# A mixture-of-experts kernel: first-choice results go through a buffer in the order of the second choices, and the output is written once

## What is computed

```python
# gnn: x + gnn(layernorm(x), adj), 128 graphs of 64 nodes, D = 128, H = 512
x = x + _L0_gnn_ref(_layernorm(x), adj, ...)
# ffn on the 8192 tokens: 8 experts, two of them per token
gate_logits = xf @ Wg + bg
top_w, top_i = jax.lax.top_k(gate_logits, 2)
top_w = jax.nn.softmax(top_w, axis=-1)
w_dense = jnp.sum(jax.nn.one_hot(top_i, E) * top_w[..., None], axis=1)
out = jnp.zeros_like(xf)
for e in range(E):
    h = jax.nn.gelu(xf @ W1[e] + b1[e], approximate=False)
    out = out + w_dense[:, e:e + 1] * (h @ W2[e] + b2[e])
```

## Time and profile before

| | us |
|---|---|
| median of 3 runs | 489.01 (488.24 to 489.42) |
| the profiled execution | 488.13 |
| its span in the trace | 486.2 |
| busy PE, PEld | 465.9 (96%), 422.8 (87%) |
| busy DVE, ACT, POOL | 354.1 (73%), 264.2 (54%), 353.4 (73%) |
| chain that ended last | PE 67%, POOL 15%, issue 14% |
| mean granted TensorE clock | 0.987 of full |

### The profile page before, as it was taken

The page is one execution under the profiler, slowest core; times in us unless marked ns, Lnnn a source line. Parts: engine busy times, 40 slices in busy tenths (PEclk is TensorE's granted clock), DMA queues, the critical chain, the costliest instruction groups (busy, mean ns, idle before and its releaser), DMA issues.

```text
span 486.2 us, 14184 instructions
## 1 busy us (share of the span) xinstructions
PE 465.9 (96%) x3715; PEld 422.8 (87%) x3715; DVE 354.1 (73%) x1484; ACT 264.2 (54%) x830; POOL 353.4 (73%) x310
## 2 busy tenths in 40 slices
PE   8999999999999999999999999999999999999960
PEld 6788888778888777899999999999999999999950
DVE  6798888888887675888867777777667676776730
ACT  2333333333333324677777777777777777777730
POOL 3232587877778777777777777777588888888884
PEclk9999999999999999999999999999999999999995
DMA  6995122222222212323334333333254555555430
GB/s 188 361 320 168 56 79 73 79 77 64 68 64 68 78 40 74 86 70 90 96 91 108 100 104 98 93 85 99 47 68 68 72 72 76 70 69 73 56 33 5
DMA packets 54436, 44.78 MB, mean 92 GB/s; under 512 B 9506, under 2 KB 46024, under 8 KB 54360
## 3 DMA queue, kind: packets, MB, share of 16 engines
q1 hardware_dynamic: 36480, 26.11, 20.0%
q0 software_dynamic: 16592, 17.13, 17.5%
q10 hardware_dynamic: 1288, 0.62, 0.4%
HBM read 25.49 MB, written 19.25 MB: 92 GB/s over the span
## 4 chain that ended last, share of the span: by engine, by line
PE 67%; POOL 15%; issue 14%; DVE 1%; ACT 1%; POOLq 1%
PE ps L683 14%; PE ps L668 14%; POOL out_y L440 14%; PE ps L589 11%; PE ps L575 10%; PE ps L541 3%; PE ps L549 3%; PE ps L582 3%; PE ps L557 2%; PE ps L661 2%; PE ps L567 1%; POOL dispatched_rows L425 1%; PE ps L500 1%; POOLq L71 1%; PE ps L612 0%
## 5 line engine op out<-in xcount | busy, mean ns | idle before, releaser
L775 ACT ACTIVATE gelu_t<-ps,block_w 128x128 f32<-128x128 f32 x568 | 162.5, 369 | 35.1 <-PE ps L668 34.7
L425 POOL DMA_INDIRECT dispatched_rows<-payload,row_idx x128 | 126.0, 985 | 37.3 <-issue 36.7
L668 PE MATMUL ps<-slot_t,block_w 128*128 128x128 f32 x1136 | 150.1, 275 | 0.6 <-ACT slot_t L769 0.6
L683 PE MATMUL ps<-experts,gelu_t 128*128 x1136 | 150.3, 275 | 0.4 <-ACT gelu_t L775 0.3
L683 PEld LDWEIGHTS ps<-experts,gelu_t 128*128 128x128 f32 x1136 | 138.2, 192 | 0.8 <-issue 0.8
L668 PEld LDWEIGHTS ps<-slot_t,block_w 128*128 128x128 f32 x1136 | 138.0, 192 | 0.9 <-ACT slot_t L769 0.9
L440 POOL DMA_INDIRECT out_y<-y_out,slot_rows x71 | 112.6, 1586 | 23.3 <-issue 23.3
L437 POOL DMA_INDIRECT out_y<-y_out,slot_rows x71 | 72.2, 1017 | 24.1 <-issue 19.0
L1115 DVE TENSOR_TENSOR y_bias<-ps,block_w 128x128 f32<-128x128 f32 x142 | 41.3, 291 | 52.8 <-PE ps L683 48.1
L1029 DVE COPY block_w<-experts 128x644 f32 x142 | 73.6, 519 | 2.0 <-issue 2.0
L1035 DVE TENSOR_SCALAR slot_n<-slot_rows 128x128 f32<-128x128 f32 x142 | 58.5, 413 | 15.5 <-DMA slot_rows<-dispatched_rows 15.1
(11 more groups left out here) (146 smaller groups left out, 413.3 us busy)
## 6 DMA issues: line engine op xcount, KB each, us to landing
slot_rows<-dispatched_rows SPq DMA_DIRECT2D x142, 66.5 KB
xs<-in_x SPq DMA_DIRECT2D x16, 256.0 KB, 6.5
xs_t<-in_x_t SPq DMA_DIRECT2D x16, 256.0 KB, 3.1
experts<-in_f_w SPq DMA_DIRECT2D x16, 256.0 KB, 5.3
out_y<-y_out,slot_rows POOLq DMA_INDIRECT x142, 3.2
adj_in<-in_adj_t SPq DMA_DIRECT2D x16, 128.0 KB, 4.3
dispatched_rows<-payload,row_idx POOLq DMA_INDIRECT x128, 2.4
dispatched_rows<-pad_rows SPq DMA_DIRECT2D x18, 66.5 KB
```

Source lines behind the costliest of these rows:

```text
L425: pool.indirect_dma_start(rows[k], bass.IndirectOffsetOnAxis(row_idx[:, g, j * TOP_K + k:j * TOP_K + k + 1], 0), payload[:, g * JT + j, 0: ...
L668: mm = pe.matmul(bank((2 * i + c // 2) % FH_BANKS, c % 2 * SLOTS, SLOTS), block_w[:, i % BLOCKS, c * P:(c + 1) * P], slot_t[:, i % 2, :], ...
L683: mm = pe.matmul(bank(Y_BANK + i % 2, 0, P), gelu_t[:, i % 2, c, :], experts[:, bass.ds(at + (OW2 + c * P), P)], start=(c == 0), stop=(c = ...
L775: act.activation(gelu_t[:, i % 2, c, :], ps[:, (2 * i + c // 2) % FH_BANKS, c % 2 * SLOTS:(c % 2 + 1) * SLOTS], ACT.Gelu, bias=block_w[:, ...
```

## The change

The payload gets one more number: PLACE, the row of the token's second choice. VectorE copies it from row_f in place_rows. A new DRAM tensor, first_results, has the rows of the second choices' regions, 128 numbers each. A first-choice tile's result (x2 included) is scattered by POOL to the rows PLACE of first_results and no longer to out. A second-choice tile loads from first_results the same 128 rows as from dispatched_rows 1, so that each row meets the earlier result of its token (SyncE, load_prior, into prior, a ring of 16 in the memory of xs, which is free by then). VectorE adds it: take_second brings the result with its bias from PSUM to y_out, and close_second multiplies by the weight and adds the prior rows. POOL then scatters to out with a plain write; every row of out is written once. wait_written is gone; in its place SyncE issues load_prior of tile 71 only behind the slots of tile 86, which wait for the write of tile 70. So that VectorE need not stand at once, the closings of tiles 71 to 77 are put off: tile 71 is closed behind the taking of tile 74, then two at a time, and from tile 78 on each tile behind its own taking.

```diff
-TOKEN, WEIGHT, MEAN, RSTD, X2 = 0, 1, 3, 4, 5
+TOKEN, PLACE, WEIGHT, MEAN, RSTD, X2 = 0, 1, 2, 4, 5, 6
...
+        first_results = nc.dram_tensor("first_results", (DUMMY + SLOTS, P), F32).ap()
...
+        prior = xs[:, 0:RING, :]
...
                 sp.dma_start(rows[g // E][bass.ds(end, SLOTS), :], pad_rows[:]).then_inc(padded, 16)
+                if g >= E:
+                    sp.dma_start(first_results[bass.ds(end, SLOTS), :], pad_rows[:, X2:WID]).then_inc(padded, 16)
...
+            def load_prior(i, first):
+                q = (i - TILES) % RING
+                sp.dma_start(prior[:, q, :], first_results[bass.ds(first, SLOTS), :]).then_inc(prior_loaded[q], 16)
...
-            for i in range(TILES, NT):
-                load_slots(i)
+            firsts = [load_slots(i) for i in range(TILES, TILES + RING)]
+            for i in range(TILES, TILES + RING):
+                load_prior(i, firsts[i - TILES])
+            for i in range(TILES + RING, NT):
+                load_prior(i, load_slots(i))
...
                 if i < TILES:
+                    place = bass.IndirectOffsetOnAxis(slot_rows[:, r, PLACE:PLACE + 1].bitcast(I32), 0)
+                    pool.indirect_dma_start(first_results, place, y_out[:, r, :], None, bounds_check=DUMMY - 1,
+                                            oob_is_err=False).then_inc(added[r], 16)
+                else:
+                    token = bass.IndirectOffsetOnAxis(slot_rows[:, r, TOKEN:TOKEN + 1].bitcast(I32), 0)
                     pool.indirect_dma_start(out, token, y_out[:, r, :], None, bounds_check=T - 1,
                                             oob_is_err=False).then_inc(added[r], 16)
-                else:
-                    pool.indirect_dma_start(out, token, y_out[:, r, :], None, bounds_check=T - 1,
-                                            oob_is_err=False, compute_op=ALU.add).then_inc(added[r], 16)
...
-                if TILES - 8 <= i < TILES - 1:
-                    wait_written(2 * i - TILES)
-                    wait_written(2 * i - TILES + 1)
-                if i == TILES:
-                    wait_written(TILES - 2)
-                    wait_written(TILES - 1)
...
+                dve.tensor_copy(payload[:, cols(g), PLACE].bitcast(I32),
+                                row_f[:].rearrange("p (j k) -> p j k", k=TOP_K)[:, :, 1])
...
+            def take_second(i):
+                r = i % RING
+                dve.wait_ge(y_done, i + 1)
+                after(dve, added[r], 16 * (i // RING))
+                dve.tensor_tensor(y_out[:, r, :], ps[:, Y_BANK + i % 2, 0:P],
+                                  block_w[:, i % BLOCKS, OB2:OB2 + P], ALU.add).then_inc(y_chain, 1)
+            def close_second(i):
+                r, q = i % RING, (i - TILES) % RING
+                dve.wait_ge(y_chain, i + 1)
+                dve.wait_ge(prior_loaded[q], 16 * ((i - TILES) // RING + 1))
+                dve.scalar_tensor_tensor(y_out[:, r, :], y_out[:, r, :],
+                                         slot_rows[:, r, WEIGHT + 1:WEIGHT + 2], prior[:, q, :],
+                                         ALU.mult, ALU.add).then_inc(y_ready, 1)
...
+                if i < TILES:
+                    finish(i)
+                else:
+                    take_second(i)
+                if i == TILES + 3:
+                    close_second(TILES)
+                if TILES + 4 <= i < TILES + 7:
+                    close_second(2 * i - TILES - 7)
+                    close_second(2 * i - TILES - 6)
+                if i >= TILES + 7:
+                    close_second(i)
```

More of the change, by code:

```diff
@@ L252, in moe_gnn @@
         added = [sem(f"added{r}") for r in range(RING)]
+        prior_loaded = [sem(f"prior_loaded{r}") for r in range(RING)]
         def q_bank(g):
@@ L331, in _ @@
                 sp.dma_start(rows[k][DUMMY:DUMMY + SLOTS, :], pad_rows[:]).then_inc(padded, 16)
+            sp.dma_start(first_results[DUMMY:DUMMY + SLOTS, :], pad_rows[:, X2:WID]).then_inc(padded, 16)
             def pad(g):
@@ L342, in load_slots @@
                              rows[i // TILES][bass.ds(first, SLOTS), :]).then_inc(slots_loaded[r], 16)
+                return first
+            def load_prior(i, first):
+                q = (i - TILES) % RING
+                sp.dma_start(prior[:, q, :], first_results[bass.ds(first, SLOTS), :]).then_inc(prior_loaded[q], 16)
             sp.wait_ge(early_table_ready, 1)
@@ L362, in _ @@
             sp.wait_ge(tables_ready, 1)
[L363 removed]
+            sp.wait_ge(padded, 16 * (E + TOP_K + 1))
             sp.wait_ge(late_dispatched, 16 * JT * (G - EARLY_GROUPS))
@@ L1119, in finish @@
                 row = slot_rows[:, r, :]
-                weight = row[:, WEIGHT + k:WEIGHT + k + 1]
-                if k == 0:
-                    m = dve.scalar_tensor_tensor(y_out[:, r, :], y_bias[:, i % 2, :], weight, row[:, X2:WID],
-                                                 ALU.mult, ALU.add)
-                else:
-                    m = dve.tensor_scalar(y_out[:, r, :], y_bias[:, i % 2, :], weight, None, ALU.mult)
-                m.then_inc(y_ready, 1)
+                dve.scalar_tensor_tensor(y_out[:, r, :], y_bias[:, i % 2, :], row[:, WEIGHT:WEIGHT + 1],
+                                         row[:, X2:WID], ALU.mult, ALU.add).then_inc(y_ready, 1)
+            def take_second(i):
+                r = i % RING
+                dve.wait_ge(y_done, i + 1)
[9 more added lines that the diff above has]
+                                         ALU.mult, ALU.add).then_inc(y_ready, 1)
             take_x2(G - 1)
@@ L1132, in _ @@
                     norm_slots(i + AHEAD)
+                if TILES < i < TILES + 8:
+                    dve.wait_ge(y_chain, i)
                 if i + 3 < NT:
```

10 lines of the change are left out of this document (2 added, 8 removed).

## The result

| | before | changed | forecast |
|---|---|---|---|
| median, us | 489.12 (16 runs, 487.3 to 492.1) | 486.87 (16 runs, 483.2 to 487.87) | 481.3 (478.8 to 485.5) |
| ratio | | 0.9937, 95% from 0.9916 to 0.9958 | 0.984 |
| profiled execution, span | 488.13, 486.2 | 486.89, 485.0 | 480.4, 478.5 |
| busy PE, DVE, POOL, us | 465.9, 354.1, 353.4 | 469.1, 353.0, 311.7 | POOL 40 less |
| mean granted clock | 0.987 | 0.989 | |

The change makes the kernel faster, by 0.6% and not by 1.6%; the time lies above the range.

A forecast was written before the change was run, and what follows sets the result against it. TensorE's matmuls set the floor, with POOL's delayed scatters behind the last one; -8.8 - 0.4 + 1.1 + 0.2 + 0.2 = -7.7 us against the 489.01 median gave 481.3, range 478.8 to 485.5.

The forecast's parts named there:

- terms a and b: Before the second choices: VectorE's copy of the place, +0.2 (0 to 0.2); eight more pad loads on SyncE, +0.2 (0 to 1).
- the new wait at the switch: VectorE waits 3.3 us for tile 71's prior rows, making TensorE about 1.0 late: +1.1 us (0 to 3.2).
- The accumulate goes, and POOL's waits with it: 71 POOL scatters each 0.57 us shorter; POOL catches up, last scatter starts at 470.45 in place of 479.28: -8.8 us.
- The rival of the clock: At the switch, TensorE still for 4.4 us drops to 1.2 GHz; ten slow tiles give about 504 us, slower; chance 0.03.
- The 4.2 us between the last landing and the end I leave as they are: End of the span: the 4.2 us after the last scatter's landing was assumed unchanged.
- The -0.4: Last scatter, issue to landing: plain write 2.4 us in the median, accumulate 2.7; -0.4 us (between -0.3 and -0.6).
- Rival 5: VectorE's closings and POOL's scatters lock each other, each waiting up to 0.98 us; about 507 us; chance 0.02.
- Rival 4: Second-choice scatters on POOL: plain costs as much as accumulating, nothing is caught up; 487 to 489 us; chance 0.03.
- term c: 71 prior-row loads on SyncE, 1.6 us a tile against 1.895, twelve tiles ahead of need: 0, covered by slack.

The follow-up runs named there:

- experiments 1 to 5: Six variants of the changed kernel: closings put off (one or four tiles more), pad loads moved, both edits, dummy matmuls, another SyncE load order; 482.51 to 489.03 us.
- before_plain: Kernel before with plain scatters for all second choices, waits kept, the addition of the two results left out; 482.84 us, ratio 0.9861.
- prior_early: Changed kernel with SyncE loading slots 71 to 80, waiting for the last six first-choice writes, then loading priors 71 to 80, then pairs from 81; 485.86 us.
- late_pads: Changed kernel with the eight pad loads of first_results moved behind the slot loads of tiles 71 to 78; 489.03 us, ratio 0.9991.
- defer7: Changed kernel with closings put off four more tiles: tile 71 closed behind the taking of tile 78; 482.51 us, ratio 0.9855.

## Why the forecast missed

The forecast span was 478.5, the changed kernel's is 485.0. The 6.5 us between, by the steps of the prediction:

| step | forecast | measured | of the 6.5 |
|---|---|---|---|
| first part, with terms a and b | +0.4 | +1.28 (taking of tile 71 at 338.86 for 337.58) | 0.9 |
| the new wait at the switch | +1.1 | +4.16 | 3.1 |
| last result to last scatter | 0.98 after the last taking | 1.56 | 0.6 |
| last scatter's start to the end | 6.9 - 0.4 = 6.5 | 8.5 | 2.0 |

1. **The accumulate goes, and POOL's waits with it** held: POOL 41.7 us less busy, last scatter nearly behind the last result. One term was too small: I took 0.30 from the last result to the last scatter, which is the step between two scatters in a backlog. POOL starts 0.79 after a result that it waits for, and here the scatter of tile 140, which runs until 476.17, makes it 0.88.
2. **The new wait at the switch** is the step that failed. The place was right, and VectorE's wait for the load is what stops TensorE; the size was a quarter of what was measured. Of the 3.1 us between, about 1.0 is the longer stop of TensorE (1.96 for 1.0), 1.7 is the clock, which I had left out of this term (see 3), and 0.4 is the rest, the wait for the weight copy above all. Two terms under the stop were wrong. I let SyncE be idle at tile 86's place in the ring, so that the landing of tile 70's write set the time (slots of 86 at 344.6); it came to them with six slot loads behind one another and issued them at 346.29, about 0.9 of the 1.7 by this backlog, 0.8 because the write itself started later (342.25 for 341.44). And I took 1.87 from issue to use where 2.8 was needed, inside my bounds (3.87); in the other profiles in which VectorE waited for this load it took 1.94 to 2.98. In the changed kernel the issuing instruction alone took 1.25, where that of the first prior load took 0.33 in all six kernels of experiments 1 to 5; nothing shows why. Together the load was usable 2.7 later than forecast; 1.2 of it is hidden, as VectorE too came later.
3. **The rival of the clock** was put in the wrong place. I wanted a gap of 4.4 us, from the one fall that the trace showed, and priced it at ten tiles of half speed. The runs show a fall behind a gap of 1.96 and one behind 3.46, each over after 3.4 us, at 1.7 us. A rival that costs 1.7 and is seen behind a stop of 2 belonged inside the main case, whose own gap was 1. The page "TensorE: Matmul & The Clock Gate" of the Trainium skill, section "Part 1: The HAM clock gate (the "warmup" mystery)", has activity release the half speed; the trace agrees in so far as TensorE had been at work from 350.25 on when the clock was full again at 354.5.
4. **"The 4.2 us between the last landing and the end I leave as they are"** was the second failed step: they were 6.4 (span end 485.0, last scatter at 476.5, and 2.1 to its landing). The -0.4 was as good as right, since the last plain scatters of before_plain and prior_early landed 2.1 after their start; the closing step, 2.17 longer without the accumulates, is what had been left out. No row of before could give this; that it is untouched was an assumption, and no bound was put on it.
5. Rival 5 fell: the closing step takes 341 to 387 ns, 352 in the median, in 71 instructions, of which 69 overlap a scatter. The rule of the Trainium skill, page "SBUF — State Buffer", section "SBUF: two separate sides", which has such a step wait for a whole instruction of POOL's, is not borne out here. Rival 4 fell with 989 ns. SyncE's new loads brought no waits after the switch (term c).

## What to carry to other kernels

When a change adds a wait on data that a queue loads, walk that queue back to its last real wait: its arrears can set the load, and not the event it nominally waits for (about 1 us of arrears in the changed kernel, 3.2 in late_pads, none in defer7). Put the consumer later until the wait is covered, since a closing that nobody but the output waits for can be late for nothing (four more tiles gave 4.4 us); and count a stop of TensorE of about 2 us nearly double, for the clock may fall behind it (1.7 more here).

## What the runs showed of the hardware that I had not expected

The clock fell not in the gap but 0.85 us after work had resumed, and stayed at 1.2 GHz for 3.4 us; it seems to have done so in ten of sixteen executions of one kernel. POOL's closing has two lengths, 5.13 to 5.17 and 7.34, on all chips alike; the short one goes with 50 or more accumulating scatters, and 21 at the end do not bring it. A plain scatter that POOL waits for starts 0.79 after the result is ready. And the first part varies by 1.9 us between profiles of kernels with the same code there, nearly the 2.25 that the change as a whole was worth.
